# Attention in an adaLN block: a group's steps set out in a hand-written table, and the sixth key block of the second query half summed by TensorE

## The reference, cut

```python
qg = q.reshape(B, N_KV_HEADS, GROUP, T, D_HEAD)
att = jnp.einsum('bhgqd,bhkd->bhgqk', qg, k) / math.sqrt(D_HEAD)
causal = jnp.tril(jnp.ones((T, T), dtype=bool))
att = jnp.where(causal[None, None, None], att, -jnp.inf)
probs = jax.nn.softmax(att, axis=-1)
ctx = jnp.einsum('bhgqk,bhkd->bhgqd', probs, v)
```

## Time and profile before

| what | value |
|---|---|
| time, median of 3 runs (lowest, highest) | 2497.97 us (2494.4, 2500.48) |
| the profiled execution's own time | 2495.66 us |
| its span, first to last instruction | 2493.9 us |
| mean granted TensorE clock | 0.990 |
| TensorE matmul busy, share of the span | 2406.7 us, 97% |
| TensorE weight load busy | 1668.3 us, 67% |
| VectorE busy | 1723.4 us, 69% |
| GpSimd busy | 1650.8 us, 66% |
| ScalarE busy | 1042.6 us, 42% |

### The profile page before, as it was taken

One profiled execution on the slowest core, in us unless ns is written; L12 is line 12 of the kernel. 1 busy time (PEld: TensorE's weight loads), 2 busy tenths in 40 slices (PEclk: granted clock), 3 DMA queues, 4 the chain that ended last, 5 costly groups with the idle time before them and its releaser, 6 DMA issues. The chain is left out here.

```text
span 2493.9 us, 36376 instructions
## 1 busy us (share of the span) xinstructions
PE 2406.7 (97%) x13140; PEld 1668.3 (67%) x13204; DVE 1723.4 (69%) x3392; ACT 1042.6 (42%) x1873; POOL 1650.8 (66%) x865
## 2 busy tenths in 40 slices
PE   5999999999999999999999999998999999999998
PEld 3788888887555555555555555544788788888886
DVE  4866666677888888888888888874555355455553
ACT  3433333231666666666666666665211111111111
POOL 3744333441799998999989999993655455545643
PEclk8999999999999999999999999999999999999999
DMA  6532333352545325344233345313333333323330
GB/s 236 198 118 87 115 113 118 123 150 80 162 100 146 82 64 154 83 132 97 71 79 83 83 117 132 84 31 127 112 92 101 103 90 97 118 86 104 107 93 25
DMA packets 179727, 267.45 MB, mean 107 GB/s; under 512 B 20508, under 2 KB 113884, under 8 KB 178400
## 3 DMA queue, kind: packets, MB, share of 16 engines
q1 hardware_dynamic: 179552, 265.13, 36.2%
HBM read 183.22 MB, written 80.81 MB: 106 GB/s over the span
## 5 line engine op out<-in xcount | busy, mean ns | idle before, releaser
L1082 POOL TENSOR_TENSOR p_sum<-p_sum,p_ring 128x1024 f32<-128x1024 f32 (+2 forms) x465 | 991.3, 2164 | 71.0 <-PE ctx_ps L1143 50.2
L976 ACT ACTIVATE p_ring<-scores 128x512 f32<-128x512 f32 (+1 forms) x896 | 448.9, 568 | 236.3 <-DVE scores L1030 173.6
L272 DVE TENSOR_REDUCE neg_max<-scores_q 128x1 f32<-128x512 f32 x679 | 438.8, 684 | 79.0 <-PE scores_q L253 64.9
L253 PE MATMUL scores_q<-k_stack,q_stack 96*128 96x512 f32 (+1 forms) x1473 | 443.0, 378 | 14.6 <-DVE neg_max L269 6.3
L1122 PE MATMUL scores<-q_stack,k_stack 98*128 98x512 f32 (+1 forms) x1216 | 409.7, 414 | 10.6 <-ACT p_ring L976 7.7
L253 PEld LDWEIGHTS scores_q<-k_stack,q_stack 96*128 96x128 f32 x1473 | 263.6, 191 | 135.4 <-DVE neg_max L269 64.5
L1122 PEld LDWEIGHTS scores<-q_stack,k_stack 98*128 98x128 f32 x1216 | 205.9, 190 | 184.7 <-ACT p_ring L976 71.9
L627 POOL TENSOR_TENSOR roped_hilo<-roped_hilo 128x512 fp32r<-128x512 f32 x80 | 105.5, 1319 | 337.0 <-ACT roped_hilo L467 337.0
L269 DVE CUSTOM_DVE_ANT_0 scores_q<-scores_q,masks 128x512 f32<-128x512 f32 x489 | 296.0, 642 | 38.4 <-PE scores_q L253 38.4
L676 PE MATMUL proj_ps<-h_hi,w_hi 128*128 128x512 f32 x752 | 298.7, 397 | 0.7 <-POOL w_lo L616 0.7
L676 PE MATMUL proj_ps<-h_hi,w_lo 128*128 128x512 f32 x752 | 294.1, 391 | 0.0
(11 more groups left out here) (182 smaller groups left out, 3632.8 us busy)
## 6 DMA issues: line engine op xcount, KB each, us to landing
q_stack<-qk_t SPq DMA_DIRECT2D x96, 512.0 KB, 6.8
qk_t<-roped_hilo SPq DMA_DIRECT2D x80, 512.0 KB, 2.8
x_in<-in_L_attn_resid SPq DMA_DIRECT2D x32, 512.0 KB, 6.3
ctx_t<-ctx_raw SPq DMA_DIRECT2D x64, 256.0 KB, 5.4
prefetched<-in_L_wmod SPq DMA_DIRECT2D x4, 4096.0 KB, 13.6
prefetched<-ctx_t SPq DMA_DIRECT2D x31, 512.0 KB, 4.0
prefetched<-inv_t SPq DMA_DIRECT2D x124, 128.0 KB, 5.5
k_stack<-qk_t SPq DMA_DIRECT2D x96, 128.0 KB, 8.8
```

The source lines that it names most:

```text
L253: last = nc.tensor.matmul(dst[:, a, :], qs[0:MHI, h, i * P:(i + 1) * P], ks[0:MHI, lo:lo + w], start=not first and (a == 0 or not diag), s ...
L272: nc.vector.tensor_reduce(neg, src, AX.X, ALU.max, negate=True).then_inc(sh.s_mx.sem, 1)
L976: nc.scalar.activation(p[:, a * per:(a + 1) * per, :], src[:, a * per:(a + 1) * per, :], ACT.Exp, scale=SM_SCALE).then_inc(s_ex.sem, 1)
L1082: nc.gpsimd.tensor_tensor(a, a, probs(n, u), ALU.add).then_inc(s_ap.sem, 1)
```

## The change

`group_steps` no longer works by rules for the maxima, the values, the sums and the turn: a table `AFTER`, one row for each unit, says word for word what follows that unit's scores. `TAIL_FROM` of half 1 falls from 7 to 6, so that unit 18 is no longer added by GpSimd (14 adds a group) and joins unit 19 in the sums product. The set of maxima made ahead of the loop stays the same (48 in all), the last group's sums stay at units 6 and 12, and the number of instructions of every other kind stays.

```diff
-TAIL_FROM = {0: 4, 1: 7}
+TAIL_FROM = {0: 4, 1: 6}
-BATCH = 2
-LAG = 2
-SUM_AT = {1: 9, 0: 16}
-AHEAD = 5
-TURN_AT = 17
-MAX_TICK = [m * NE // NM - AHEAD for m in range(NM)]
+AFTER = [
+    [],
+    maxima(1, 10, 11) + quads(-1, 10, 11) + maxima(1, 12, 13),
...
+    maxima(1, 18) + quads(0, 1) + sums_of(-1, 1) + maxima(1, 19, 20),
...
+    maxima(2, 4, 5) + quads(0, 7) + turned(1) + maxima(2, 6),
...
+]
@@ def group_steps(n):
-        for at, t in ((n + 1, u), (n + 2, u - NE)):
-            if at < NG:
-                steps += [("max", at, m) for m in range(NM) if MAX_TICK[m] == t]
-        for hf in range(2):
-            at = n - 1 if hf else n
-            if u == (SUM_AT if n < NG - 1 else SUM_AT_LAST)[hf] and 0 <= at < NG:
-                steps.append(("sum", at, hf))
-        if n + 1 < NG and u == TURN_AT:
-            steps.append(("turn", n + 1))
+        for step in AFTER[u]:
+            at = n + step[1]
+            if 0 <= at < NG and not (step[0] == "sum" and n >= NG - 1):
+                steps.append((step[0], at) + step[2:])
+        if n >= NG - 1:
+            for hf in range(2):
+                if u == SUM_AT_LAST[hf] and 0 <= n - hf < NG:
+                    steps.append(("sum", n - hf, hf))
```

More of the change, by code:

```diff
@@ L99, with maxima, quads, sums_of @@
 QUARTER = D // 4
-MAX_TICK = [m * NE // NM - AHEAD for m in range(NM)]
+def maxima(ahead, *units):
+    return [("max", ahead, m) for m in units]
+def quads(ahead, *quads):
+    return [("values", ahead, q) for q in quads]
+def sums_of(ahead, hf):
+    return [("sum", ahead, hf)]
+def turned(ahead):
+    return [("turn", ahead)]
+AFTER = [
+    [],
+    maxima(1, 10, 11) + quads(-1, 10, 11) + maxima(1, 12, 13),
+    maxima(1, 14),
+    maxima(1, 15) + quads(0, 0) + maxima(1, 16),
+    maxima(1, 17),
+    maxima(1, 18) + quads(0, 1) + sums_of(-1, 1) + maxima(1, 19, 20),
+    maxima(1, 21, 22),
+    maxima(1, 23),
+    maxima(1, 24, 25) + quads(0, 2, 3) + maxima(1, 26),
+    maxima(1, 27, 28),
+    maxima(1, 29) + quads(0, 4) + maxima(1, 30, 31),
+    [],
+    maxima(1, 32, 33, 34) + quads(0, 5) + maxima(1, 35),
+    maxima(1, 36, 37),
+    maxima(2, 0),
+    maxima(2, 1, 2) + quads(0, 6) + sums_of(0, 0) + maxima(2, 3),
+    [],
+    maxima(2, 4, 5) + quads(0, 7) + turned(1) + maxima(2, 6),
+    maxima(2, 7),
+    maxima(2, 8, 9) + quads(0, 8, 9),
+]
+EARLY = [s[2] for r in AFTER for s in r if s[0] == "max" and s[1] == 2]
 def group_steps(n):
@@ L129, in group_steps @@
                 steps.append(({MOD_AT: "mod", MOD_OUT: "mod_out", MOD_IN: "mod_in"}[u], i))
-        at, v = (n, u - LAG) if u >= LAG else (n - 1, u - LAG + NE)
-        if 0 <= at < NG and v == QUADS[QUAD_OF[v]][-1] and QUAD_OF[v] % BATCH == BATCH - 1:
-            steps += [("values", at, q) for q in range(QUAD_OF[v] - BATCH + 1, QUAD_OF[v] + 1)]
     return steps
 STEPS = [s for n in range(NG + 1) for s in group_steps(n)]
-FIRST_MAXIMA = [(0, m) for m in range(NM)] + [(1, m) for m in range(NM) if MAX_TICK[m] < 0]
+FIRST_MAXIMA = [(0, m) for m in range(NM)] + [(1, m) for m in EARLY]
 UNIT_AT = {}
```

## The result

The changed kernel takes 2431.78 us (median of 4 runs, 2427.48 to 2435.28), the kernel before 2497.69 beside it (2494.4 to 2500.48): a ratio of 0.9736, 95% interval 0.9716 to 0.9756. Two later series gave 2436.03 and 2433.17 us.

What follows compares the result with a forecast made beforehand. TensorE was taken as the bound, losing about 2.5 us of each 33.50 us group to stalls. 31.0 + 0.44 + 0.25 + 0.25 = 31.95; over 30 groups -46.5, last group -2.3, giving 2449 us, range 2436 to 2478.

Steps and rivals of the forecast that it cites:

- stalls which its busy time hides: TensorE in a steady group: about 2.5 us of 33.50 lost waiting, though recorded busy 32.87; all expected back.
- 31.0 us of work: TensorE's own work in an old steady group, once about 2.5 us of stalls leave the 33.50.
- m12 and m13: Two maxima ahead of a values block: took 0.83 us where 0.62 is needed, so 0.2 lost.
- m2, m3 and m18 leave the crowded stretch: Units 16 to 4, where maxima meet diagonal masks: VectorE falls from 12.9 to 11.2 us, 105% to 87% of TensorE's need.
- the long values block or the bunch of maxima is split: Single quads of 0.88 us between maxima remove each listed stall's cause, so all 2.5 us come back.
- unit 18 in the sums product: TensorE gains a 256-wide piece for four heads, +0.44 us a group; GpSimd loses one 2.34 us add.
- work, with one more block of 32-column products: TensorE per group: 31.0 us, plus 0.25 (0 to 0.5) for switches as eight blocks and a turn become nine.
- wait for the rows: Unit 0 waits for the turned maxima's rows to land, 3.75 us after the turn against 3.5: +0.25 (0 to 0.55).
- lost to VectorE: Steady group after the change: no stall behind VectorE left, 0 us.
- The ring: Half 1's sums product to quad 4, then GpSimd's adds, back to that product: 31.6 us; 33.9 with unit 18 on GpSimd.
- The last group: TensorE's 2.45 us wait for GpSimd's last add shrinks as one 2.34 us add goes: -2.3 us once.
- What would show it: Signs: groups of 31.7 to 32.2 us, weight-load waits for VectorE under 20 from 57, VectorE near 90%, GpSimd idle 2.

Runs made afterwards that it cites:

- halved reductions: VectorE reduces only the first half of each maximum's columns: on the kernel before, 2452.3 us (group 31.65); on the changed kernel, 2428.43 us (group 31.42).
- the tail piece alone: Kernel before with unit 18 moved from GpSimd into the sums product, old order kept: 2509.83 us, ratio 1.0042.
- the table alone: Changed kernel with unit 18 back on GpSimd, the table's order kept: 2517.59 us, ratio 1.0077 against the kernel before.

## Why the prediction was right in its mechanism, and where its sizes failed

**That the old group held stalls which its busy time hides** was the step everything stood on, and it held: halved reductions took 1.85 us out of a group that showed 0.63 us of idle time. The size, 2.5 us, was somewhat too small. The forecast's 31.0 us of work was got by subtracting stalls from 33.50, and a place left out of the list, or put at an estimate, counts as work. One such place is m12 and m13: they took 0.83 and were allowed 0.62, and with halved reductions they take 0.57 in the same place (1021.50 to 1022.07).

**The cause** was told half right. "m2, m3 and m18 leave the crowded stretch" names the sum over a stretch, and with just that done the group went to 36.7 us. The clause behind it, "the long values block or the bunch of maxima is split", was the mechanism: with three banks the distance between maxima counts, at the scale of one or two reductions. That a 1.6 us sums product taken from between m18 and m19 costs 0.6 us a group shows the same from the other side. The forecast said it in half a sentence and put its arithmetic in the other half.

**The terms of the steady group.** The forecast's sum was 31.0 + 0.44 + 0.25 + 0.25 = 31.95; measured is 31.52.

| term | forecast, us | shown by the runs, us |
|---|---|---|
| unit 18 in the sums product | +0.44 | +0.45 (that edit alone) |
| work, with one more block of 32-column products | 31.0 + 0.25 | 30.90, worked out below |
| wait for the rows | +0.25 | +0.14 (1.78 for 1.64 from the last two quads to unit 0) |
| lost to VectorE | 0 | +0.03 (halved reductions, with rows and ring taken out) |

31.52 less 0.45, 0.14 and 0.03 is 30.90. The reading of the old order without its stalls gave 30.95, which leaves nothing for the additional block, within the error of a reading. **The term that failed in the steady group is thus the work, with the switches, over-put by 0.35 us**, and beside it the wait for the rows by 0.11. The rows' wait was mis-sized by the start of the copy: ScalarE began it 0.55 us after the turn, and the forecast took about 0.74, from an exponential that was to end 0.7 after it. How the 0.35 splits between work and switches no run here separates.

**The ring** held as a mechanism and nearly as a number: 31.6 us forecast, and it binds at 31.42 with the halved reductions. It leaves room by about a tenth in the steady group of the changed kernel. With unit 18 in it the kernel is slower than before, by the clock. Where it binds in the changed kernel is in groups in which GpSimd has other work, which the forecast did not look at. GpSimd's and TensorE's timelines of the changed kernel, in group 26 and 27:

```profile
1494.51 2.38 POOL L1115 TENSOR_TENSOR prefetched<-prefetched 128x1024 f32<-128x1024 f32 x1
```

```profile
1514.54 1.06 PE L1204 MATMUL scores_q<-p_sum,ones_v 128*32 128x512 f32 x8 [2.01 <-POOL p_sum L1111]
```

One operation of 2.38 us between the adds comes back as 2.01 us of TensorE's wait, and the group takes 33.73. In the other two profiled executions of the changed kernel the same wait was followed by 3.4 us at a clock of 0.50, and the group took 35.37. The stretch behind it in the first of these two, whose mean clock is 0.57:

```profile
1510.07:1514.00 3.93, 3.93 (x29) 1.99 (x29) 0.39 (x1) 0.59 (x1) 3.76 (x3) 0.57 0.00 0
```

Such groups are why 0.43 us less in a steady group did not bring 13 us: the 31 periods up to the last group add up to 1059.6 us before and 1008.1 after, 51.5 less, where 31 times 1.98 is 61.4. Of the 10 that are missing, 2.9 are GpSimd's, in groups 27 and 29. Late rows take 0.8 to 1.1 us in each of four groups. In the nine groups of the other kinds the halved reductions won 7 us back, some of it from rows that no longer landed late; how the rest divides between rows and VectorE is not separated.

**The last group** was forecast 2.3 us shorter and is 7.0 shorter (38.3 to 31.35). The step read one wait in it, 2.45 us for GpSimd. TensorE's timeline of that group before has, beside it, waits for exponentials, of which two stand here:

```profile
1685.21 1.55 PE L1122 MATMUL scores<-q_stack,k_stack 98*128 98x512 f32 x3 [0.43 <-ACT p_ring L976]
...
1713.60 1.27 PE L1122 MATMUL scores<-q_stack,k_stack 98*128 98x512 f32 x3 [0.70 <-ACT p_ring L976]
```

and after it has one, of 0.22 us:

```profile
1652.98 0.98 PE L1151 MATMUL scores<-q_stack,k_stack 98*128 98x512 f32 x2 [0.22 <-ACT p_ring L1005]
```

The clock comes on top. Two stretches of the last group of the kernel before, and the whole of it in the kernel with the tail piece alone:

```profile
1685.00:1687.00 2.00, 1.79 (x7) 0.85 (x11) 1.13 (x3) 1.45 (x5) 2.00 (x2) 0.76 0.35 131
1687.00:1690.00 3.00, 3.00 (x20) 0.71 (x16) 0.49 (x1) 1.43 (x3) 3.00 (x3) 0.59 0.00 0
```

```profile
1701.00:1738.02 37.02, 34.71 (x270) 14.16 (x270) 5.90 (x12) 21.11 (x43) 8.78 (x5) 0.91 0.04 16
```

0.76 over 2 us and 0.59 over 3 are 1.7 us of work lost; 0.91 over 37.0 is 3.3 lost, so that the 1.3 us which the tail piece alone wins there are 2.9 without the clock. Of these the forecast's -2.3 is the 2.45 of the wait less the 0.44 that the longer sums product costs here too, 2.0; the forecast left the 0.44 out. In the changed kernel the clock is 1.00. The 7.0 us are thus 2.0 for GpSimd, 1.8 of waits for exponentials (five of 0.22 to 0.70 us, 2.05 together, for one of 0.22), 1.7 of clock, and 1.5 whose place is not shown. There are no maxima in the last group to fill the time of the exponentials; a single quad with its sums between pairs of units does. The experiment that moved quads and sums alone has the last group at 31.4, so it is these and not the maxima's places. **The other step that failed is the last group's term, -2.3 for -7.0**: it was costed for the tail piece, and the new order was left out of it.

**The account.** Of the profiled execution's 60.4 us, 51.5 lie in the groups (46.5 forecast), 7.0 in the last group (2.3), 5.0 in the output half, which is not changed and in the profiled executions of this study took between 766 and 775 us (the kernel before has the 775), and attention began 3.1 us later, at a point that varied from 620.7 to 626.9. So 9.7 us of the miss are found in the groups and the last group, more than the 4 us by which the time lies below the range. The output half's 5.0, and the distance of the two profiled executions from their medians (2 us below it before, 3.5 above after), are differences between executions for which I have no cause.

**What would show it.** The period of 31.52 lies just below the band of 31.7 to 32.2; GpSimd's gap ahead of unit 8's add is 1.55 us for about 2, VectorE is at 93% for about 90. The weight loads' wait for VectorE, to fall from 57 us to under 20, fell to 33.4 on its line and rose on the other: a wrong sign to look for, where the start-to-start distance had to fall. The page of the Trainium skill that the prediction drew on (Perfetto Trace Analysis, Identifying the Most-Contended Engine) ranks the weight load's busy share above the matmul's. Here that share rose from 53% to 58% of a group (17.83 of 33.50 us, 18.17 of 31.52) and did point to room in the old group, but how much room it did not say.

## What to carry to other kernels

When an in-order engine alternates between work that fills a few buffers and work that does not, place the second kind between pieces of the first, at the scale of one buffer's emptying; a balance over a longer stretch is no guide, and moving the first kind alone was here worse than moving nothing, while moving the second alone brought about half of the gain. Cost such an order by start-to-start distances, since neither the busy share nor the waits of the weight load say what a stall costs. Look separately at the last round of a loop and at the rounds that carry extra work, where the fill is different and a ring with a tenth of slack binds; and where a ring does bind by 2 us a round, reckon with TensorE's clock as well as with the wait. When a variant is run to price one engine's lateness, look whether another wait has gone, or another ring has begun to bind, in the same run.

## What the runs showed of the hardware that I had not expected

- A weight load's recorded wait was no measure of loss: 257 waits and 126 us for VectorE's reductions in the changed kernel; halving the reductions gave back some 5 us of time, 10 in the groups of the profiled execution.
- In the kernel with the table alone TensorE waits 24 times for over 2 us (most 2.2); behind 21 of these waits the granted clock was 0.50 after 1.00 ahead of them; a stretch of 3.4 us at half speed lengthened the group by 1.6 us, one of 6.4 by 2.9. Other waits of that length were followed by 1.00: 2.01 us in the changed kernel (1514.54 us), 2.45 in the last group of the kernel before (1694.35), where it fell at 1685 to 1690 us behind shorter ones. At the same place of the same program, group 27 of the changed kernel, it stayed up in one execution and fell in two. The length of the wait alone does not decide it.
- The change of kind between score or maximum products and 32-column blocks was steady to a hundredth or two of a us: 0.32 for the last maximum ahead of a block (0.235 within a row of maxima), 1.00 for a single quad (0.88 within a block), and 0.34 for the product behind it.
- GpSimd's adds were not slowed by a denser VectorE: 2.38 us for one of 1024 columns with VectorE busy 93% of the group.
